# Rows for the experts gathered by a node list instead of scattered into regions

## The reference, cut to what matters

```
gate_scores = x @ Wg + bg                       # x: the normed rows, 6250 x 256; 8 experts
_, idx = jax.lax.top_k(gate_scores, 2)
mask = jax.nn.one_hot(idx, 8).sum(axis=-2)
h = gelu(einsum('td,edh->teh', x, W1) + b1)     # 512 hidden per expert
y = einsum('teh,ehd->ted', h, W2) + b2
out = einsum('ted,te->td', y, mf)               # mf: the mask; no gate weight
```

## Time and profile before

| | |
|---|---|
| median of 3 runs | 4109.37 us (4106.85 to 4113.02) |
| the profiled execution | 4104.44 us, its span 4102.8 us |
| PE busy | 2951.5 us (72%) |
| PEld busy | 2101.5 us (51%) |
| DVE busy | 2469.6 us (60%) |
| ACT busy | 1236.8 us (30%) |
| POOL busy | 1585.3 us (39%) |
| mean granted TensorE clock | 0.841 |

### The profile page before, as it was taken

The page is one execution under the profiler, slowest core; times in us unless marked ns, Lnnn a source line. Parts: engine busy times, 40 slices in busy tenths (PEclk is TensorE's granted clock), DMA queues, the critical chain, the costliest instruction groups (busy, mean ns, idle before and its releaser), DMA issues. The chain is left out here.

```text
span 4102.8 us, 67269 instructions
## 1 busy us (share of the span) xinstructions
PE 2951.5 (72%) x20826; PEld 2101.5 (51%) x20827; DVE 2469.6 (60%) x7438; ACT 1236.8 (30%) x2741; POOL 1585.3 (39%) x1664
## 2 busy tenths in 40 slices
PE   2541788886988888483048885149999996998798
PEld 2440455553664555273047774126776774666444
DVE  6956888773444443466124444669887773678454
ACT  1202122331421001031123332136554441433554
POOL 1010777771027777321721112656555442333000
PEclk9655689998989999786579997559999998898899
DMA  4103444442035554354421112653333225011000
GB/s 136 77 29 120 128 144 135 159 158 75 23 123 159 160 159 143 112 174 160 143 83 62 66 64 81 209 189 107 99 99 89 82 81 173 29 42 37 27 23 27
DMA packets 242287, 429.53 MB, mean 105 GB/s; under 512 B 34308, under 2 KB 181303, under 8 KB 236825
## 3 DMA queue, kind: packets, MB, share of 16 engines
q0 software_dynamic: 71904, 196.05, 16.0%
q1 hardware_dynamic: 155552, 175.03, 13.0%
q10 hardware_dynamic: 14620, 55.77, 3.7%
HBM read 313.04 MB, written 113.68 MB: 104 GB/s over the span
## 5 line engine op out<-in xcount | busy, mean ns | idle before, releaser
L1132 POOL DMA_INDIRECT scr<-xn_table,src_i x392 | 373.5, 953 | 340.3 <-PE psum L977 221.1
L1132 POOL DMA_INDIRECT scr<-h_table,src_i x392 | 371.5, 948 | 326.5 <-issue 324.4
L1132 POOL DMA_INDIRECT xnT<-xn_table,src_i x392 | 375.2, 957 | 257.5 <-issue 222.2
L977 PE MATMUL psum<-scr 128*128 128x128 f16 (+1 forms) x3136 | 318.5, 259 | 89.0 <-issue 82.1
L977 PEld LDWEIGHTS psum<-scr 128*128 128x128 f16 (+1 forms) x3136 | 297.4, 153 | 131.3 <-issue 99.2
L759 ACT ACTIVATE scr<-scr,agg 128x128 f16<-128x128 f16 x710 | 252.2, 395 | 80.3 <-DVE scr L742 73.7
L2756 PE MATMUL psum<-scr,xnT 128*128 128x128 f16 x2544 | 198.8, 234 | 64.2 <-issue 58.6
L984 DVE SCALAR_TENSOR_TENSOR agg<-psum,agg 128x256 f32 (+1 forms) x196 | 95.1, 485 | 234.5 <-PE psum L971 215.0
L740 DVE TENSOR_SCALAR scr<-iota,agg 128x128 f16<-128x128 bf16 x710 | 223.9, 318 | 9.0 <-PEq L3044 9.0
L789 PE MATMUL psum<-xnT,agg 128*128 128x512 f16 x637 | 223.9, 389 | 0.6 <-DVE agg L726 0.6
L2756 PEld LDWEIGHTS psum<-scr,xnT 128*128 x2544 | 177.6, 104 | 82.4 <-issue 68.9
(11 more groups left out here) (499 smaller groups left out, 7063.8 us busy)
## 6 DMA issues: line engine op xcount, KB each, us to landing
adjacency_table<-agg ACTq DMA_DIRECT2D x13, 1568.0 KB, 6.3
scr<-adjacency_table ACTq DMA_DIRECT2D x13, 1568.0 KB, 7.5
scr<-expert_rows SPq DMA_DIRECT2D x106, 128.0 KB, 2.0
expert_results<-scr POOLq DMA_DIRECT2D x106, 128.0 KB, 2.1
scr<-xnT_table SPq DMA_DIRECT2D x98, 128.0 KB, 3.1
xnT<-xnT_table SPq DMA_DIRECT2D x2, 5376.0 KB, 22.6
agg<-in_L_ffn_W SPq DMA_DIRECT2D x16, 512.0 KB, 9.7
x_table<-scr SPq DMA_DIRECT2D x14, 512.0 KB, 3.1
```

The lines of the kernel that those rows point to most:

```text
L977: last = pe.matmul(bank[b][:, s, :], lhs, hot[:, hot_b, t, :], start=(t == 0 and n == 0), stop=(t == CT - 1 and n == pieces - 1))
L1132: g.indirect_dma_start(out=rows[:, u, t, :], out_offset=None, in_=table, in_offset=bass.IndirectOffsetOnAxis(ap=index(t), axis=0)).then_in ...
```

## The change

`send_to_experts` is replaced by `list_expert_nodes`. In `route` the scatter rows, the pad rows and the first rows of tiles are no longer computed; instead the place of each node is split into its tile and its row within the tile (`slot_tile`, `slot_row`). The new stage turns these into a list `node_of`: for each of the 106 tiles and 128 rows, the number of the node that belongs there (0 where nothing does). VectorE makes two one-hot tables for each choice and node tile, one of the row (128 wide) and one of the tile (106 wide) times the node's number, and TensorE adds up the 98 products of such pairs in one PSUM bank. The weights are split beside it as before. In `experts` GpSimd gathers the 128 rows of a tile straight from `xn2_tab` by the list, and SP stores the results.

```
-REGION = NP + P
...
-        self.slot_x = dram("expert_rows", (EXPERTS * REGION, D))
...
+        self.slot_tile, self.slot_row = slots.take([2, NT]), slots.take([2, NT])
+        self.node_of = slots.take([MT], I32)
...  route, VectorE
             for n in range(2):
...
-                do(v.tensor_scalar(start_of, code[n], -float(REGION), float(EXPERTS * REGION), ALU.mult, ALU.add))
-                do(v.tensor_tensor(c.scatter_to[:, n, :], start_of, rank_of[n], ALU.add))
...
-            do(v.tensor_scalar(where, rev, -float(REGION), float(EXPERTS * REGION), ALU.mult, ALU.add))
-            do(v.tensor_tensor(where, where, upto[:, :, NT - 1], ALU.add))
-            do(v.tensor_scalar(c.pad_to[:], where, node[:, 0:1], None, ALU.add))
+            do(v.tensor_scalar(place, c.result_at[:], 7, None, ALU.arith_shift_right))
+            do(v.tensor_copy(c.slot_tile, place))
+            do(v.scalar_tensor_tensor(c.slot_row, c.slot_tile, -float(P), c.result_at[:], ALU.mult, ALU.add))
...
-            do(v.memset(t_row, 0.0))
             for e in range(EXPERTS):
...
-                do(v.tensor_scalar(later, tile_no, first[:, e:e + 1], None, ALU.subtract))
-                do(v.tensor_scalar(later, later, float(P), float(e * REGION), ALU.mult, ALU.add))
-                do(v.tensor_tensor(later, later, inside, ALU.mult))
-                do(v.tensor_tensor(t_row, t_row, later, ALU.add))
             do(v.tensor_copy(c.tile_expert[:], t_expert))
-            do(v.tensor_copy(c.tile_row[:], t_row))
...  the new stage, in place of send_to_experts
+    table = c.psum[:, 2, 0:MT]
+    turns = [(n, s) for n in range(2) for s in range(NS)]
...
+        def _(g):
+            g.iota(node, pattern=[[P, NT]], base=0, channel_multiplier=1,
+                   allow_small_or_imprecise_dtypes=True).then_inc(numbered, 1)
...
+        def _(v):
+            v.wait_ge(numbered, 1)
+            for i, (n, s) in enumerate(turns):
+                if i >= 2:
+                    v.wait_ge(used, i - 1)
+                for j in range(TS):
+                    t = s * TS + j
+                    v.tensor_scalar(row_hot[:, i % 2, j, :], c.iota[:], c.slot_row[:, n, t:t + 1], None, ALU.is_equal)
+                    last = v.tensor_scalar(tile_hot[:, i % 2, j, :], c.iota[:, 0:MT], c.slot_tile[:, n, t:t + 1],
+                                           node[:, t:t + 1], ALU.is_equal, ALU.mult)
+                last.then_inc(hot, 1)
+                if i < EXPERTS:
+                    for k, (w, parts) in enumerate(((w1, c.w1_16), (w2, c.w2_16))):
+                        v.wait_ge(high, 2 * i + k + 1)
+                        v.scalar_tensor_tensor(parts[:, i, :, 1, :], w[:, i, :, :], WS, parts[:, i, :, 0, :],
+                                               ALU.mult, ALU.subtract)
+            v.wait_ge(used, len(turns))
+            v.tensor_copy(c.node_of, table)
...
+        def _(pe):
+            for i in range(len(turns)):
+                pe.wait_ge(hot, i + 1)
+                for j in range(TS):
+                    last = pe.matmul(table, row_hot[:, i % 2, j, :], tile_hot[:, i % 2, j, :],
+                                     start=(i == 0 and j == 0), stop=(i == len(turns) - 1 and j == TS - 1))
+                last.then_inc(used, 1)
...  experts, SP
-            def load(i, b):
-                row = sp.value_load(c.tile_row[0:1, ds(i, 1)], min_val=0, max_val=EXPERTS * REGION - P)
-                sp.dma_start(x[:, b, :], c.slot_x[ds(row, P), :]).then_inc(x_ready[b], 16)
+            with sp.Fori(0, MT // 2) as q:
+                for b in range(2):
+                    sp.wait_ge(y_out, q * 2 + b + 1)
+                    sp.dma_start(c.slot_y[ds((q * 2 + b) * P, P), :], y[:, b, :]).then_inc(stored[b], 16)
             for b in range(2):
-                load(b, b)
...
+                sp.wait_ge(stored[b], 16 * (MT // 2))
             sp.wait_ge(loaded, c.constants.at(16))
...  experts, GpSimd
-            with gp.Fori(0, MT // 2) as q:
...
-                    gp.dma_start(c.slot_y[ds((q * 2 + b) * P, P), :], y[:, b, :]).then_inc(stored[b], 16)
...
+            for i in range(MT):
+                if i >= 2:
+                    gp.wait_ge(turned, i - 1)
+                gp.indirect_dma_start(out=x[:, i % 2, :], out_offset=None, in_=c.xn2_tab,
+                                      in_offset=bass.IndirectOffsetOnAxis(ap=c.node_of[:, i:i + 1], axis=0)
+                                      ).then_inc(x_ready[i % 2], 16)
```

More of the change, by code:

```diff
@@ L2399, in route @@
     picked, rank_of = part.take(T8), [part.take([NT]), part.take([NT])]
-    start_of = part.take([NT])
+    start_of, place = part.take([NT]), part.take([2, NT], I32)
     count_i, ntile = part.take([EXPERTS], I32), part.take([EXPERTS])
@@ L2428, in _ @@
             g.iota(rev, pattern=[[-1, EXPERTS]], base=EXPERTS, channel_multiplier=0, **small).then_inc(const, 1)
[L2429 removed]
             g.iota(tile_no, pattern=[[1, MT]], base=0, channel_multiplier=0, **small).then_inc(const, 1)
             g.memset(tri, 1.0).then_inc(const, 1)
[L2433 removed]
+            g.wait_ge(const, 3)
             g.affine_select(out=tri, in_=tri, compare_op=ALU.is_gt, fill=0.0, base=0, pattern=[[1, P]],
@@ L2526, in send_to_experts @@
     part.at = EXPERTS * HM * D
-    rows = part.take([2, 4, D])
-    zero_rows = part.take([D])
-    to = part.take([2, 2, 4], I32)
+    part.words = SCR - 4 * NT - MT
+    row_hot, tile_hot = part.take([2, TS, P]), part.take([2, TS, MT])
+    node = part.take([NT])
     raw = c.agg.rearrange("p a b -> p (a b)")
@@ L2537, in send_to_experts @@
     w2 = raw[:, words:2 * words].rearrange("p (e k n) -> p e k n", k=HM, n=D)
-    zero, landed = c.sem("pad_rows_zeroed"), [c.sem(f"send_rows_landed{h}") for h in range(2)]
-    idx_ready, begun, sent = c.sem("send_indices_ready"), c.passed, [c.sem(f"rows_sent{h}") for h in range(2)]
+    numbered, hot, used = c.sem("nodes_numbered"), c.sem("slot_hots_made"), c.sem("slot_hots_used")
     high = c.sem("weights_high")
-    PADS = (16 * EXPERTS, 0)
+    table = c.psum[:, 2, 0:MT]
+    turns = [(n, s) for n in range(2) for s in range(NS)]
     with nc.Block() as block:
[L2545 to L2562, removed]
+        @block.gpsimd
+        def _(g):
+            g.iota(node, pattern=[[P, NT]], base=0, channel_multiplier=1,
+                   allow_small_or_imprecise_dtypes=True).then_inc(numbered, 1)
         @block.scalar
         def _(a):
[L2566 to L2569, removed]
             for e in range(EXPERTS):
@@ L2573, in _ @@
                     a.activation(parts[:, e, :, 0, :], w[:, e, :, :], ACT.Copy, scale=WS).then_inc(high, 1)
[L2574 to L2596, removed]
@@ new lines, in _ @@
+        @block.vector
+        def _(v):
[16 more added lines that the diff above has]
+            v.tensor_copy(c.node_of, table)
@@ L2599, in experts @@
+        @block.tensor
+        def _(pe):
[5 more added lines that the diff above has]
+                last.then_inc(used, 1)
 def experts(c):
@@ L2660, in _ @@
         def _(gp):
-            with gp.Fori(0, MT // 2) as q:
-                for b in range(2):
-                    gp.wait_ge(y_out, q * 2 + b + 1)
-                    gp.sem_inc(c.passed, 1)
-                    gp.dma_start(c.slot_y[ds((q * 2 + b) * P, P), :], y[:, b, :]).then_inc(stored[b], 16)
-            for b in range(2):
-                gp.wait_ge(stored[b], 16 * (MT // 2))
+            for i in range(MT):
[4 more added lines that the diff above has]
+                                      ).then_inc(x_ready[i % 2], 16)
         @block.scalar
@@ L4009 @@
 PHASES = (make_constants, prepare_edges, count_degrees, list_edges, scale_by_degrees, gather_first, first_conv,
-          gather_second, fold_attention, first_layer_sum, route, send_to_experts, experts, second_norm, gather_third,
+          gather_second, fold_attention, first_layer_sum, route, list_expert_nodes, experts, second_norm, gather_third,
           fold_second_attention, second_layer_sum, gates, second_mixture)
```

21 lines of the change are left out of this document (8 added, 13 removed).

## The result

The changed kernel takes 3991.99 us (median of four runs, 3982.84 to 3995.47) against 4109.09 us (four runs, 4106.85 to 4113.02): ratio 0.971, 95% interval 0.9696 to 0.9725, that is 117.1 us less. The forecast was 3996 us, in a range of 3982 to 4026.

A forecast was written before the change was run, and what follows sets the result against it. Stages run one after another, each bound by its last engine: GpSimd in sending, TensorE in experts, then GpSimd's drain. Terms -10.7 - 92.2 - 1.5 - 9.1 = -113.5 us from the 4109.4 median gave 3995.9; range 3982 to 4026.

The forecast's parts named there:

- TensorE's share of the listing: Listing stage: seven products per turn take 1.6 us against 3.1 on VectorE, so they lie beside it.
- Route: Route stage: removed VectorE steps 11.4 us, added 0.75, net -10.7 us, ending at 1916.9, still behind SP.
- Listing: New stage replacing the sending of rows: VectorE needs 62.7 us, stage 66.0 against 158.2, -92.2 us.
- Rival (a): Listing stage: slow tables, VectorE's pairs take their own lengths without overlap, +18 us, 4014; chance 0.10.
- the tail of 2.1 us: Listing's end: only the last turn's products show, 1.6 us and 0.3 for the pipe's end.
- The experts' start: Head of the experts: gather starts at once on GpSimd beside the bias, -1.5 us, between 0 and -3.
- The experts' loop: Experts' tiles: gather cycle of 2.7 to 6.4 us hidden in some 6.3, so 0; other bound +37.
- The experts' end: End of the experts: GpSimd's 8.7 us drain lies under TensorE's last tiles, -9.1 us.
- Rival (d): End of the experts: the drain still closes the stage despite the change, 4005 us; chance 0.07.
- (b): Experts' loop: late gathers, each landing at 6.7 us, 0.35 per tile, +37 us, 4033; chance 0.08.
- (c): Experts' loop: VectorE holds GpSimd's gathers, cycle 9.7 against 6.3 us, 180 over 106 tiles, 4176; chance 0.03.

The follow-up runs named there:

- e6: Changed kernel with each product of the listing stage made twice and the sum halved when copied: 3995.01 us, ratio 0.9736.
- e7: Changed kernel with a turn's tables made in two wide VectorE compares, ScalarE multiplying in the node numbers: 3979.88 us, ratio 0.9693.
- e0: The changed kernel run once more, unaltered, beside the kernel before: 3990.7 us, ratio 0.9708.
- e5: Changed kernel with the 1 MB load of the experts' bias moved into the listing stage: 3989.08 us, ratio 0.9709.
- e3: Changed kernel without the gather, SP loading plain tiles in node order: 3987.45 us, ratio 0.970.
- e1: Kernel before with only the stores of the last four expert tiles moved from GpSimd to SP: 4094.04 us, ratio 0.9961.
- e2: Changed kernel with only the store of the last expert tile given back to GpSimd: 3999.77 us, ratio 0.9729.
- e4: Changed kernel with each gather released one tile later than its buffer is free: 4051.21 us, ratio 0.9867.

## Why the prediction was right

It was right by its own steps: route, listing and the experts' end came by the mechanisms named and within 1.3 us each. Three readings were off. TensorE's share of the listing was taken at half, which by chance did not reach the time; the experts' start was taken 1.7 us too short and their loop 2.2.

**Route**, -10.7 forecast and -10.7 measured: VectorE still ends it, and SP was done at 1911.9, ahead of the barrier at 1916.95.

**Listing**, -92.2 forecast (66.0 us), -93.5 measured (64.7). VectorE was to need 62.7 us and was busy for 61.76; drain and barrier are short. The rule of the Trainium skill that I had weighed (VectorE: DVE Perf Modes, The DRAIN you can't avoid), read as no overlap between operations that follow each other, would have made it 84; the rows show starts 0.19 to 0.25 us apart where one operation lasts 0.28 or 0.33. Rival (a) is out with that.

The mis-sized step is TensorE's: "Seven per turn are 1.6 us against 3.1 on VectorE, so they lie beside it". I took the earlier trace rows for eight products; the changed kernel has 196 instructions for 98 products, two for each, so those eight were four (L3169 of the kernel before makes four calls). A turn is 14 instructions, 3.32 us at a clock of 0.50, against VectorE's 3.08. TensorE was thus not half as busy as VectorE but level with it. It cost next to nothing for two reasons. In the first eight turns VectorE also has its two subtractions, 2.27 us, and TensorE idles 2.03 us per turn. Then come turns without subtractions; there TensorE was last by a hair (VectorE waited 0.3 us for it in all), ran without a stop for 6.30 us, and then got the 2.4 GHz level for two turns (1.81 us each) and, after a turn back at 1.2, for most of the last. So the tail of 2.1 us, forecast as 1.9, came out by an accident. At 1.2 GHz it would have been 3.3 and 0.3. e6 and e7 show the same from both sides: more products, or cheaper tables, and TensorE is what is waited for.

**The experts' start**, -1.5 forecast, +0.2 measured (first product 5.4 us after the stage's start before, 5.6 after; 5.2 in e0, so nothing clear of the executions). The term held the thought that the gather "starts at once on GpSimd, beside the bias", and that a step of SP's chain goes away. It does start, 0.9 us into the stage, but it shares the rings with a megabyte of bias, and e5 shows the price: 4.75 us to the product instead of 2.76. Moving the load off SP's chain gave nothing that shows; the bytes ahead of it had stayed.

**The experts' loop**, 0 forecast, bounds 0 to +37. From the first product to the last rows it was 438.6 us before and is 440.8 after, +2.2. It is not the gather: e3 has none and shows 440.4. Nor is it measured by any one wait: TensorE's stops for the expert numbers grew from 58.6 to 60.3 us, but e1 has 61.6 of them with the short loop. Nor is it the granted clock, which is 0.91 over the loop before, in after and in e6, whose loop took 440.3. e1, which has the stores of 102 tiles still on GpSimd and loads on SP, shows 438.4. What the changed kernel, e2 and e3 have in common is that SP stores nearly all rows; whether that is the cause of 2 us was not tried, and stays open.

**The experts' end**, -9.1 forecast, -9.6 measured (last rows to barrier 11.8 us before, 2.2 after), by the mechanism named: the drain now lies under TensorE's last tiles. It started 23 us ahead of the barrier, where 18 to 22 were expected. Rival (d) is out, and e1 and e2 show that the term stands where GpSimd has the last transfer, and not where SP has it.

**Rivals (b) and (c).** Both needed a cycle from release to full tile over 6.3 us; e4 measured 3.2 at the median and 4.7 at the longest. The hold that (c) rests on is real where it was seen before: in the second norm a gather took 13.44 us again (2437.86 to 2451.30, its row is above). It lay under the same clearing and under the TENSOR_TENSOR that follows it without a gap, and ended 0.8 us after that:

```profile
2436.82 7.74 DVE L2860 MEMSET agg<- 128x9216 f32 x1 [1.72 <-issue]
2444.49 6.00 DVE L2864 TENSOR_TENSOR scr<-iota,agg 128x5680 f32<-128x5680 f32 x1
```

(The Trainium skill, SBUF — State Buffer, Who interferes with whom, names copy, cast and tensor_scalar as the forms that can take the two-port modes which block GpSimd, and says that a tensor_tensor with both inputs in SBUF contends with GpSimd's reads. A clearing is not among the forms that it names for this chip, so these 13.44 us go beyond its rule.) In the experts' loop 106 gathers, spread beside VectorE's steps over 425 us, show nothing of it: 0.974 us at most (1.29 in e4). They do meet VectorE at work:

```profile
2242.16 0.94 POOL L2635 DMA_INDIRECT scr<-xn_table,scr  x1 [2.45 <-PE psum L2712]
2242.17 0.45 DVE L2678 TENSOR_SCALAR scr<-scr 128x512 f16<-128x512 f32 x1
...
2242.66 0.69 DVE L2680 SCALAR_TENSOR_TENSOR scr<-scr 128x512 f16<-128x512 f32 x1
```

So VectorE at work beside a gather does not by itself hold it; whether the form of its work or its length decides was not tried.

**Sum.** The forecast of -113.5 us stands against -117.1 between medians. Of the three stages with an edit, the profiled pair shows -111.4: 10.7, 93.5 and 7.2. The some +2.4 between that and the pair's -109.0 are the untouched stages, the last one's clock above all. That the medians came within 4 us of the forecast is therefore in part luck: the stages gave 2 us less than it, and the executions, which differ by more than that, the rest.

## What to carry to other kernels

Ask of each stage what its last engine must still do when the last data are through: here a drain of 9 us was taken off the path by giving the last transfers to another queue, which the sequencers' rows at the block ends showed and no table of busy time did. When a step is costed at nothing because another engine covers it, count instructions and not calls, and at the clock level that the engine will have there: a cover of half may be a tie. To measure what is hidden, take its cover away by one step (the gather one tile later): the stage then grows, and its length can be read.

## What the runs showed of the hardware that was not expected

- GpSimd's drain goes on after its last transfer instruction has ended, and it is no fixed price. Counted from the end of GpSimd's last instruction (or from the drain's start where that is later) it was 8.7 us after 106 scatters, stores or gathers, 8.4 after 102 stores (e1), 8.8 after 107 transfers (e2: 106 gathers and the one store), and 8.1 after the 98 gathers of the second norm, whose drain is the longest of these because gathers were still running when it began:

```profile
L2800 POOLq DRAIN  x1: 16068/16068/16068, 2591.9 to 2591.9; - x1
```

  So it grew with the number of the block's transfers, but not by one rule for all: it was 2.6 to 2.9 after 18 gathers of the edge lists and 6.6 to 7.6 after the 392 of an edge stage. In the blocks of route, listing and e3's experts, with no transfer by GpSimd, the drain took 0.04 to 0.40. SP's took 0.007. What GpSimd does in that time no run shows.
- An f32 product of 128x128 by 128x106 is two instructions on TensorE, some 0.21 us apart at 1.2 GHz (14 in 3.3 us) and 0.11 at 2.4 GHz (14 in 1.8 us).
- Twice the products cost 1.9 us, while TensorE's granted clock rose with them from 0.57 (after) to 0.82 (e6) over the listing: in the turns at the 2.4 GHz level 28 instructions took 3.37 us, where 14 had taken 3.32 at 1.2.
- The last stage, the same in all kernels, took 278.2 to 287.2 us in the profiled executions, and the longer, the lower the clock that TensorE was granted in it (0.99 to 0.95).
